# Block sums kept in PSUM banks and rotary products of 512 columns in an attention block, and the first pair's copy of P1 issued earlier

## The chip, the core and the metric

One core of a Trainium2 chip. The program is one launch; the metric is device time in microseconds of that core, median of 3 runs. Engines are named as in the profile: PE is TensorE (PEld its weight loads), DVE VectorE, ACT ScalarE, POOL GpSimd, SP SyncE, which issues loads.

## The reference, cut to what matters

```python
x = x + attn(cond(x, ids1, W1, b1, lora_As, lora_Bs), wq, wk, wv, wo)
x = x + ffn(cond2(x, ids2, W2, Wr2, A2, B2), base_w, base_b, A, Bf, router_w)

def attn(x, wq, wk, wv, wo):                     # 32 query heads, 8 key/value heads, head_dim 128, S = 64
    q, k, v = (x @ wq), (x @ wk), (x @ wv)       # reshaped to heads
    q, k = rope(q, pos), rope(k, pos)            # [t1 cos - t2 sin, t1 sin + t2 cos]
    scores = einsum("bqhgd,bshd->bhgqs", q, k) * head_dim ** -0.5
    attn = softmax(where(causal, scores, min))   # per key/value head g
    return einsum("bhgqs,bshd->bqhgd", attn, v).reshape(B, S, 4096) @ wo
```

x is 32 sequences of 64 tokens of width 1024, all in float32.

## The kernel before, in words

Tokens lie along the free axis and features along the partitions. The 2048 tokens are worked in two halves of 1024 (two tiles t = 0, 1 of NT = 512 columns), by one loop `hf` over the whole program of each engine. Each engine has its own hand-written instruction stream; nothing but semaphores orders one against another. Every float32 operand of a product is split into a high and a low part, and a product is three matmuls (`three`, L713 to L715): high by high, high by low, low by high.

The stage that the change touches lies between the first projection and the product with wo. It works through 24 pairs of heads per half (`pair(B, lp)`). Their kind goes round in threes: KV (one key and one value head), Q01 and Q23 (two query heads each). A pair is a 2 x 2 block product of Strassen's kind: seven products P1, P6, P2, P5, P7, P4, P3 in this order on PE, each 12 matmuls of 512 columns into one of four PSUM banks `prod0` to `prod3` (`BANK`: P1 and P2 share bank 2, P6 and P7 bank 3, P5 and P3 bank 1, P4 has bank 0). DVE joins them to the four result blocks: C11 = P1 + P2 lies complete in bank 2 after P2, U2 = P1 + P6, U3 = P1 + (P6 + P7), C22 = U3 + P5, C21 = U3 - P4, C12 = U2 + (P5 + P3). C11 and C12 are the two token tiles of the pair's first head, C21 and C22 those of the second. ACT makes the copy of P1 (`p1_copy`, L1339, tile `p_sum`) which U2 and U3 need; P2 overwrites nothing but adds to the same bank, so PE waits for that copy before P2.

The weights of the seven products go to seven slots: POOL forms sums of blocks (L1592), ACT rounds them to the high part (L1260, `weight_hi`), POOL subtracts for the low part (L1597).

Keys and query heads are then turned (rope): per piece two products with sin on 64 partitions each (L1901, to `rope_sin`), one with cos (L1903), and their sum (L1905) into `k_rot` or `q_rot`. Value heads are transposed on PE instead (`turn_v`).

Attention of a pair of query heads, in two units of one token tile each, is spread over the next two pairs: PE puts `score` of the first unit (16 matmuls, L897) ahead of the next pair's P6, the second one's ahead of P5, the transpose `turn_p` (L909) of the first ahead of P4 and its product with V (`pv`, L922) ahead of P3, and the second unit's at the start of the pair after. DVE masks the scores and takes the maximum (`before_exp`, L1860 to L1865), ACT takes the exponential (L1358), DVE scales (`normalise`, L1872 and L1874).

In the first pair of each half P4 needs T4, a sum that DVE makes in three steps over 2048 columns (L1839, L1841, L1844), ACT rounds (L1331) and DVE splits (`t4_lo`, L1848).

Of the kernel before, what the change touches and what calls it, by code (L numbers as in the profile page):

```python
# [130 lines left out]
def raw_count(r):  # L131
# [16 lines left out]
U2, C11, U3, C22, C21, C12 = range(1, 7)  # L148
NC = 6
# [6 lines left out]
          "s_sum": 5 * PAIRS, "unit": 4 * NKV, "tb": 6 * NKV, "qk": 8 * NKV, "raw": 16 * PAIRS // 2,  # L156
          "stored": 16 * 2 * NKV, "head": 0}
A_LOOP = {k: v * PAIRS_IT // PAIRS for k, v in A_STEP.items()}
A_LOOP["head"] = 2 * GQ
C_N = 2 * KC  # L160
# [6 lines left out]
def build(nc, x, ids1, ids2, W1, b1, A1, B1, wq, wk, wv, wo, W2, Wr2, A2, B2, Wf, bf, Af, Bf, Rf, consts,  # L167
          gates_d, m_d, c2_d, t_d, x1_d, o_d, out):
    assert D == TOK and KC == TB
    with ExitStack() as ctx:  # L170
# [161 lines left out]
        comb = sem("comb")  # L332
        roped = sem("rope_products")
# [367 lines left out]
        def _(pe):  # L701
# [83 lines left out]
            with pe.Fori(0, HALVES) as hf:  # L785
# [104 lines left out]
                def score(B, u):  # L890
# [3 lines left out]
                    pe.wait_ge(qk_in, B["qk"] + (8 * lg + 2 + 3 * (w // 2) + 2 + t))  # L894
# [32 lines left out]
                def attention(B, lp, n):  # L927

                    if lp % 3 != Q01 and lp >= 2:
                        e = 4 * ((lp - 1) // 3) + 2 * (lp % 3 == KV)  # L930
                        if n == 1:
                            score(B, e)
                        if n == 3:
                            score(B, e + 1)
                        if n == 5:
                            turn_p(B, e)
                        if n == 6:
                            pv(B, e)
                    if lp % 3 != Q23 and lp >= 3:
                        e = 4 * ((lp - 2) // 3) + 2 * (lp % 3 == Q01)  # L940
                        if n == 0:
                            turn_p(B, e + 1)
                        if n == 1:
                            pv(B, e + 1)
# [3 lines left out]
                def pair(B, lp):  # L948

                    for n in range(NP):  # L950
# [40 lines left out]
                def group(gd, par, first=False):  # L991
# [4 lines left out]
                    for i in range(32):  # L996
# [9 lines left out]
                        if first and i < 4:  # L1006

                            pe.wait_ge(comb, hf * A_STEP["comb"] + (A_STEP["comb"] - NC + (C11, U3, C21, C12)[i] + 6))
# [148 lines left out]
        def _(act):  # L1157
# [49 lines left out]
            with act.Fori(0, HALVES) as hf:  # L1207
# [1064 lines left out]
```

## Time and profile before

| | us |
|---|---|
| median of 3 runs (lowest to highest) | 2933.24 (2920.47 to 2942.37) |
| the profiled execution's own time | 2936.61 |
| its span, first to last instruction | 2934.7 |
| PE busy in the span | 2784.2 (95%) |
| DVE, POOL, ACT busy | 1770.2, 1154.9, 842.9 |
| mean granted TensorE clock, as a share of full speed | 0.964 |

The two attention stages of pairs lie at about 289 to 950 us and 1683 to 2346 us of the span. In the profile page's timeline of 40 slices PE is at 8 tenths in a few slices there and at 9 nearly everywhere else. The chain of work that ended last is 82% PE and 9% DVE.

### The profile page before, as it was taken

How to read it: one execution, taken by the hardware profiler on the slowest of the kernel's cores; microseconds unless marked ns; L12 is line 12 of the kernel's file. 1: busy time of each engine (PE TensorE's matmuls, PEld its weight loads, DVE VectorE, ACT ScalarE, POOL GpSimd, SP SyncE). 2: the span in 40 equal slices, each digit the busy share in tenths (PEclk: the TensorE clock that was granted, in tenths of full speed). 3: DMA queues.
4: the chain of work that ended last, by engine and by line, in shares of the span. 5: the costliest groups of instructions: out<-in, count | busy, mean ns of one | idle time of the engine just before them, and what ended most of it. 6: DMA issues, size and time to landing. Idle time of an engine off the chain costs nothing.

```text
span 2934.7 us, 40314 instructions
## 1 busy us (share of the span) xinstructions
PE 2784.2 (95%) x13368; PEld 2272.3 (77%) x13368; DVE 1770.2 (60%) x2187; ACT 842.9 (29%) x2019; POOL 1154.9 (39%) x678
## 2 busy tenths in 40 slices
PE   8989799999999999999998889999999999999999
PEld 7867677877777888887877667787777788887887
DVE  2133677677776766655524467767877676566452
ACT  2133234333333321121103333343333322112110
POOL 0020776666775122210303276766667412221030
PEclk9999899999999999999999999999999999999999
DMA  6861122211212332221444112212122332321232
GB/s 209 232 177 41 52 72 64 68 59 58 72 56 93 140 108 92 89 70 52 112 140 123 43 44 72 73 58 72 52 65 66 114 122 97 105 93 51 70 101 68
DMA packets 280502, 260.00 MB, mean 89 GB/s; under 512 B 67706, under 2 KB 217338, under 8 KB 280322
## 3 DMA queue, kind: packets, MB, share of 16 engines
q1 hardware_dynamic: 235106, 202.11, 23.3%
q10 hardware_dynamic: 45216, 55.58, 5.4%
q8 instruction: 102, 1.67, 0.2%
q14 instruction: 78, 0.64, 0.1%
HBM read 193.49 MB, written 64.16 MB: 88 GB/s over the span
## 4 chain that ended last, share of the span: by engine, by line
PE 82%; DVE 9%; issue 4%; POOL 2%; SPq 1%; DMA 1%; ACT 1%; DVEq 0%; POOLq 0%; ACTq 0%
PE prod L713 24%; PE prod L715 23%; PE prod L714 23%; PE turned L897 5%; DVE rope_sin L1901 2%; DVE q_rot L1903 2%; DVE q_rot L1905 2%; PE turned L922 2%; PE turned L707 1%; PE prod L1144 1%; PE turned L909 1%; POOL slot_f L1592 1%; DVE combined L1940 1%; POOL slot L1597 1%; PE prod L811 1%
## 5 line engine op out<-in xcount | busy, mean ns | idle before, releaser
L1997 DVE TENSOR_TENSOR x<-prod,x 128x512 f32<-128x512 f32 x512 | 346.8, 689 | 256.9 <-PE prod L715 256.3
L1636 POOL TENSOR_TENSOR w_lo<-raw,w_hi 128x1024 fp32r<-128x1024 f32 x64 | 157.0, 2452 | 578.1 <-ACT w_hi L1419 578.1
L713 PE MATMUL prod<-c_hi,slot 128*128 128x512 f32 x768 | 310.0, 404 | 27.6 <-ACT p_sum L1339 26.5
L713 PE MATMUL prod<-c_hi,w_hi 128*128 128x512 f32 (+1 forms) x832 | 327.3, 393 | 3.4 <-DVE c_lo L2021 3.4
L715 PE MATMUL prod<-c_hi,w_lo 128*128 128x512 f32 (+1 forms) x832 | 324.2, 390 | 0.0
L714 PE MATMUL prod<-c_lo,w_hi 128*128 128x512 f32 (+1 forms) x832 | 323.8, 389 | 0.0
L715 PE MATMUL prod<-c_hi,slot 128*128 128x512 f32 x768 | 301.5, 393 | 0.0
L714 PE MATMUL prod<-c_lo,slot 128*128 128x512 f32 x768 | 301.2, 392 | 0.0
L713 PE MATMUL prod<-x_hi,w_hi 128*128 128x512 f32 x656 | 283.4, 432 | 7.6 <-DVE w_lo L1739 2.1
L1597 POOL TENSOR_TENSOR slot<-slot_f,slot 128x512 fp32r<-128x512 f32 x144 | 212.6, 1476 | 135.4 <-ACT slot L1260 135.4
L1358 ACT ACTIVATE probs<-probs,row_max 128x64 f32<-128x64 f32 x512 | 171.0, 335 | 301.6 <-DVE row_max L1865 301.6
L715 PE MATMUL prod<-x_hi,w_lo 128*128 128x512 f32 x656 | 257.6, 393 | 0.0
L714 PE MATMUL prod<-x_lo,w_hi 128*128 128x512 f32 x656 | 256.9, 392 | 0.0
L713 PE MATMUL prod<-t_hi,slot 128*128 128x512 f32 x576 | 254.2, 441 | 1.2 <-DVE t_lo L1848 1.2
L714 PE MATMUL prod<-t_lo,slot 128*128 128x512 f32 x576 | 238.5, 414 | 0.0
L715 PE MATMUL prod<-t_hi,slot 128*128 128x512 f32 x576 | 238.5, 414 | 0.0
L897 PE MATMUL turned<-k_rot,q_rot 128*128 128x64 f32 x1024 | 151.6, 312 | 80.9 <-DVE q_rot L1905 80.9
L1901 DVE TENSOR_TENSOR rope_sin<-combined,consts_sb 64x512 f32<-64x512 f32 (+1 forms) x160 | 220.0, 1375 | 10.9
L897 PEld LDWEIGHTS turned<-k_rot,q_rot 128*128 128x128 f32 x1024 | 147.9, 226 | 96.1 <-issue 93.4
L713 PE MATMUL prod<-o_xhi,w_hi 128*128 128x512 f32 x512 | 199.3, 389 | 0.0
L715 PE MATMUL prod<-o_xhi,w_lo 128*128 128x512 f32 x512 | 199.2, 389 | 0.0
L714 PE MATMUL prod<-o_xlo,w_hi 128*128 128x512 f32 x512 | 199.2, 389 | 0.0
(176 smaller groups left out, 5328.7 us busy)
## 6 DMA issues: line engine op xcount, KB each, us to landing
o_scratch<-o_f ACTq DMA_DIRECT2D x64, 512.0 KB, 2.8
raw<-in_wo SPq DMA_DIRECT2D x64, 512.0 KB, 3.4
raw<-t_scratch SPq DMA_DIRECT2D x34, 512.0 KB, 3.5
raw_a<-in_wq SPq DMA_DIRECT2D x32, 512.0 KB, 4.7
raw<-in_wq SPq DMA_DIRECT2D x32, 512.0 KB, 4.8
c_lo_f<-o_scratch SPq DMA_DIRECT2D x32, 512.0 KB, 5.0
o_xf<-o_scratch SPq DMA_DIRECT2D x32, 512.0 KB, 5.4
t_scratch<-x ACTq DMA_DIRECT2D x17, 512.0 KB, 5.0
```

The costliest lines, as they stand in the source:

```text
L713: pe.matmul(dst, wh, xh, start=start, stop=False, skip_group_check=skip)
L714: pe.matmul(dst, wh, xl, start=False, stop=False, skip_group_check=skip)
L715: return pe.matmul(dst, wl, xh, start=False, stop=stop, skip_group_check=skip)
L897: mm = pe.matmul(SCB[:, b * SEQ:(b + 1) * SEQ], Q[:, t * 2 * NT + b * P:t * 2 * NT + (b + 1) * P], K[:, t * NT + b * SEQ:t * NT + (b + 1) ...
L922: mm = pe.matmul(OB[par][:, b * P:(b + 1) * P], V[rows, (t * BPT + b) * HD:(t * BPT + b + 1) * HD], PT[rows, b * P:(b + 1) * P], start=Tru ...
L1358: ins = act.activation(SM[:, c:c + SEQ], SM[:, c:c + SEQ], ACT.Exp, bias=MX[:, m:m + 1], scale=SM_SCALE, accum_out=SUM[:, m:m + 1])
L1597: pool.tensor_tensor(slot_lo(n), src, slot_hi(n).bitcast(F32), ALU.subtract).then_inc(s_lo, 1)
L1636: pool.tensor_tensor(WL[j % 2][:], RAW[j % 2][:], WH[j % 2][:].bitcast(F32), ALU.subtract).then_inc(split_d, 1)
L1901: dve.tensor_tensor(view(rs[a:a + hd2, :], segs), x[b:b + hd2], sin, ALU.mult)
L1903: dve.tensor_tensor(out, x, cos, ALU.mult).then_inc(signal, 1)
L1905: dve.tensor_tensor(out, out, view(rs, segs), ALU.add).then_inc(qk_in, 1)
L1997: dve.tensor_tensor(X1[:, xs], PJ[q % 4][:], X1[:, xs], ALU.add).then_inc(taken, 1)
```

## The change: what it does

Three things are changed in the pair stage.

1. For pairs of query heads, C22 is written into PSUM bank 3 and C21 into bank 0 instead of the SBUF tile `combined`; for all pairs C12 is written into bank 1. Only a value head's two blocks still go to `combined`.
2. Every rope is now of 512 columns: two per key head as before, four per pair of query heads instead of two of 512 and one of 1024 (`rope` replaces `turn`). Its source is always a PSUM bank; the product with cos overwrites that bank, after a wait for the products with sin, and the last sum reads the bank and `rope_sin`, which has two buffers in turn. C21 and C22 are turned in two ropes, C21 first.
3. Because a bank is free only when its rope is through, PE's waits ahead of P1, P6, P5 and P4 of the next pair (and ahead of the first four products of the stage after) go by `qk_in`, the count of finished ropes, instead of `comb`. Only the pairs after a KV pair keep `comb` for P6 and P4. The scores wait for the rope they need: of the first tile for the second rope, of the second tile for the fourth.

Beside that, in the first pair of each half: ACT issues `p1_copy` right after the rounding of P2's weights and not after those of P5, P7, P4, of T4 and of P3's weights; DVE makes the third step of T4 after U2 and not before it. And `attention` on PE is written with tables: where a late unit's pv and a score stand ahead of the same P6, the pv now comes first.

```diff
-U2, C11, U3, C22, C21, C12 = range(1, 7)
-NC = 6
+U2, U3, C22, C21, C12 = range(1, 6)
+NC = 5
+R11, R21, R22, R12 = range(1, 5)
...
+        def qk_count(lp, n=0):
+            return 10 * (lp // 3) + (0, 2, 6)[lp % 3] + n + 4
...
 # PE: score(B, u)
-                    pe.wait_ge(qk_in, B["qk"] + (8 * lg + 2 + 3 * (w // 2) + 2 + t))
+                    pe.wait_ge(qk_in, B["qk"] + qk_count(3 * lg + 1 + w // 2, R12 if t else R21))
...
 # PE: pair(B, lp), ahead of each product but P2
-                            last = {P1: C11 - NC, P6: U3 - NC, P5: C12 - NC, P4: C21 - NC, P7: U2, P3: C22}[n]
-                            pe.wait_ge(comb, B["comb"] + (NC * lp + last + 6))
+                            if n in (P7, P3):
+                                pe.wait_ge(comb, B["comb"] + (NC * lp + {P7: U2, P3: C22}[n] + 6))
+                            elif lp % 3 == Q01 and n in (P6, P4):
+                                pe.wait_ge(comb, B["comb"] + (NC * (lp - 1) + {P6: U3, P4: C21}[n] + 6))
+                            elif lp % 3 == Q01:
+                                pe.wait_ge(qk_in, B["qk"] + qk_count(lp - 1, {P1: 1, P5: 2}[n]))
+                            else:
+                                pe.wait_ge(qk_in, B["qk"] + qk_count(lp - 1, {P1: R11, P6: R22, P5: R12, P4: R21}[n]))
...
 # ACT, first pair of a half
-                for n in (P2, P5, P7, P4):
-                    weight_hi(B0, 0, n)
-                act.wait_ge(t4_step, hf * 4 + 3)
-                act.copy(T4H[:], T4LF[:]).then_inc(t4_hi, 1)
-                weight_hi(B0, 0, P3)
...
+                weight_hi(B0, 0, P2)
+                p1_copy(B0, 0)
+                for n in (P5, P7, P4):
+                    weight_hi(B0, 0, n)
+                act.wait_ge(t4_step, hf * 4 + 3)
+                act.copy(T4H[:], T4LF[:]).then_inc(t4_hi, 1)
+                weight_hi(B0, 0, P3)
...
 # DVE
+                    def rope(out, x):
+                        n = done[0]
+                        done[0] += 1
+                        rs = view(RS[:, (n % 2) * NT:(n % 2 + 1) * NT], SPT)
+                        x = view(x, SPT)
+                        if lp or n >= 2:
+                            dve.wait_ge(qk_in, B["qk"] + qk_count(lp, n - 1))
                         for a, b in ((0, hd2), (hd2, 0)):
-                            dve.tensor_tensor(view(rs[a:a + hd2, :], segs), x[b:b + hd2], sin, ALU.mult)
-                        dve.tensor_tensor(out, x, cos, ALU.mult).then_inc(signal, 1)
-                        dve.wait_ge(signal, value)
-                        dve.tensor_tensor(out, out, view(rs, segs), ALU.add).then_inc(qk_in, 1)
+                            ins = dve.tensor_tensor(rs[a:a + hd2], x[b:b + hd2], sin, ALU.mult)
+                        ins.then_inc(turned_sin, 1)
+                        dve.wait_ge(turned_sin, B["qk"] + (qk_count(lp, n + 1) - 4))
+                        dve.tensor_tensor(x, x, cos, ALU.mult).then_inc(roped, 1)
+                        dve.wait_ge(roped, B["qk"] + (qk_count(lp, n + 1) - 4))
+                        dve.tensor_tensor(out, x, rs, ALU.add).then_inc(qk_in, 1)
...
-                    dve.tensor_tensor(b1_, b0, bank[P5], ALU.add).then_inc(comb, 1)
+                    dve.tensor_tensor(b1_ if kind == KV else bank[P7], b0, bank[P5], ALU.add).then_inc(comb, 1)
...
-                    dve.tensor_tensor(b0, b0, bank[P4], ALU.subtract).then_inc(comb, 1)
+                    dve.tensor_tensor(b0 if kind == KV else bank[P4], b0, bank[P4], ALU.subtract).then_inc(comb, 1)
                     if kind != KV:
                         combined(C21)
-                        turn(1, both, view(CB[:, 2 * NT:4 * NT], TT * SPT), TT * SPT, 0, roped, r_of(B, lp, 1))
+                        rope(dst[0][1], bank[P4])
+                        rope(dst[1][1], bank[P7])
                     formed(P3)
-                    dve.tensor_tensor(a1, a1, bank[P3], ALU.add).then_inc(comb, 1)
+                    dve.tensor_tensor(bank[P3], a1, bank[P3], ALU.add).then_inc(comb, 1)
                     combined(C12)
-                    turn(1 if kind == KV else 2, dst[1], view(a1, SPT), SPT, 0, roped, ...)
+                    rope(dst[1][0], bank[P3])
```

DVE's stream at the end of a pair of query heads, from the sum C21 to the last rope, before (`combined` is the SBUF tile, `prod` a PSUM bank; "waits" names the semaphore of an instruction's wait):

```order
L1940 TENSOR_TENSOR combined<-combined,prod 128x512 [waits comb]
L1901 TENSOR_TENSOR rope_sin<-combined,consts_sb 64x1024 [waits qk_in]
L1903 TENSOR_TENSOR q_rot<-combined,consts_sb 128x16x64
L1905 TENSOR_TENSOR q_rot<-q_rot,rope_sin 128x16x64 [waits rope_products]
L1946 TENSOR_TENSOR combined<-combined,prod 128x512 [waits a_prod]
L1901 TENSOR_TENSOR rope_sin<-combined,consts_sb 64x512 [waits qk_in]
L1903 TENSOR_TENSOR q_rot<-combined,consts_sb 128x8x64
L1905 TENSOR_TENSOR q_rot<-q_rot,rope_sin 128x8x64 [waits rope_products]
```

The same place in the changed kernel (each `rope_sin` row stands twice in both kernels and is shown once; the rope of C22 reads like that of C21, its first row is shown):

```order
L1965 TENSOR_TENSOR prod<-combined,prod 128x512 [waits comb]
L1921 TENSOR_TENSOR rope_sin<-prod,consts_sb 64x512 [waits qk_in]
L1925 TENSOR_TENSOR prod<-prod,consts_sb 128x512 [waits turned_sin]
L1927 TENSOR_TENSOR q_rot<-prod,rope_sin 128x8x64 [waits rope_products]
L1921 TENSOR_TENSOR rope_sin<-prod,consts_sb 64x512 [waits qk_in]
L1971 TENSOR_TENSOR prod<-combined,prod 128x512 [waits a_prod]
```

The one rope of 1024 columns has become two of 512, and no rope instruction reads two SBUF tiles any longer.

ACT's stream at the first pair of a half, before, from the rounding of P2's weights (`slot_96`) on:

```order
L1260 CAST slot_96<-raw_88 128x512 [waits c_prod,a_raw0]
L1260 CAST slot_97<-slot_f_104 128x512 [waits s_sum]
L1260 CAST slot_98<-slot_f_105 128x512 [waits s_sum]
L1260 CAST slot_99<-raw_89 128x512 [waits c_prod,a_raw1]
L1331 CAST t_hi<-t_lo_f 128x2048 [waits t4_step]
L1260 CAST slot_100<-slot_f_107 128x512 [waits s_sum]
L1339 COPY p_sum<-prod 128x512 [waits comb]
```

And in the changed kernel:

```order
L1274 CAST slot_96<-raw_88 128x512 [waits c_prod,a_raw0]
L1346 COPY p_sum<-prod 128x512 [waits comb]
L1274 CAST slot_97<-slot_f_104 128x512 [waits s_sum]
L1274 CAST slot_98<-slot_f_105 128x512 [waits s_sum]
L1274 CAST slot_99<-raw_89 128x512 [waits c_prod,a_raw1]
L1441 CAST t_hi<-t_lo_f 128x2048 [waits t4_step]
L1274 CAST slot_100<-slot_f_107 128x512 [waits s_sum]
```

The copy of P1 has moved ahead of five rounding steps, the rest keeps its order.

## Rows read from the trace of the kernel before

**Rows 1.** Waits: who waited for whom, us in total, times, longest.

```profile
PE turned L897 <- DVE q_rot L1905: 80.9, 30, 3.7
PE prod L713 <- ACT p_sum L1339: 26.5, 2, 13.2
```

**Rows 2.** Windows: length; busy PE, PEld, DVE, ACT, POOL; clock; DMA.

```profile
289.00:950.00 661.00, 605.55 (x3095) 498.99 (x3094) 483.22 (x517) 244.99 (x767) 446.47 (x285) 0.93 0.21 65
950.00:1555.00 605.00, 596.60 (x2706) 484.17 (x2704) 344.81 (x502) 119.53 (x166) 106.88 (x42) 0.99 0.33 102
1683.00:2346.00 663.00, 610.27 (x3111) 503.18 (x3112) 476.78 (x521) 248.32 (x776) 445.65 (x284) 0.93 0.22 67
```

**Rows 3.** Timeline of PE: start, duration, line, tiles, [idle before <- releaser].

```profile
504.44 0.39 PE L715 MATMUL prod<-t_hi,slot 128*128 128x512 f32 x1
...
513.99 3.67 PE L897 MATMUL turned<-k_rot,q_rot 128*128 128x64 f32 x16 [3.34 <-DVE q_rot L1905]
...
517.99 0.63 PE L714 MATMUL prod<-t_lo,slot 128*128 128x512 f32 x1
...
524.42 1.89 PE L897 MATMUL turned<-k_rot,q_rot 128*128 128x64 f32 x16
...
544.02 3.31 PE L897 MATMUL turned<-k_rot,q_rot 128*128 128x64 f32 x16 [1.72 <-DVE q_rot L1905]
```

**Rows 4.** Timeline of DVE, from C21 of a Q01 pair to its last rope.

```profile
504.95 0.69 DVE L1940 TENSOR_TENSOR combined<-combined,prod 128x512 f32<-128x512 f32 x1 [1.22 <-PE prod L715]
505.76 3.61 DVE L1901 TENSOR_TENSOR rope_sin<-combined,consts_sb 64x1024 f32<-64x1024 f32 x2
509.38 2.22 DVE L1903 TENSOR_TENSOR q_rot<-combined,consts_sb 128x1024 f32<-128x1024 f32 x1
511.63 2.17 DVE L1905 TENSOR_TENSOR q_rot<-q_rot,rope_sin 128x1024 f32<-128x1024 f32 x1
...
517.18 1.67 DVE L1903 TENSOR_TENSOR q_rot<-combined,consts_sb 128x512 f32<-128x512 f32 x1
518.88 0.69 DVE L1905 TENSOR_TENSOR q_rot<-q_rot,rope_sin 128x512 f32<-128x512 f32 x1
```

**Rows 5.** Timeline of POOL in the same stretch, two rows that follow each other.

```profile
516.58 1.72 POOL L1597 TENSOR_TENSOR slot<-raw_a,slot 128x512 fp32r<-128x512 f32 x1
524.52 1.28 POOL L1597 TENSOR_TENSOR slot<-s_f,slot 128x512 fp32r<-128x512 f32 x1 [6.22 <-ACT slot L1260]
```

**Rows 6.** Groups by form: count, busy us, mean ns, idle before.

```profile
L897 PE MATMUL turned<-k_rot,q_rot 128*128 128x64 f32 x1024 | 151.6, 312 | 80.9 <-DVE q_rot L1905 80.9
...
L1901 DVE TENSOR_TENSOR rope_sin<-prod,consts_sb 64x512 f32<-64x512 f32 x96 | 66.1, 688 | 97.8 <-PE prod L715 96.9
...
L1903 DVE TENSOR_TENSOR q_rot<-prod,consts_sb 128x512 f32<-128x512 f32 x32 | 22.1, 692 | 0.4
```

**Rows 7.** Timeline of all engines in the first pair of half 1.

```profile
297.17 2.54 POOL L1597 TENSOR_TENSOR slot<-slot_f,slot 128x512 fp32r<-128x512 f32 x1 [0.73 <-ACT slot L1260]
298.62 3.24 DVE L1844 TENSOR_TENSOR t_lo_f<-t_hi_f,t_lo_f 128x2048 f32<-128x2048 f32 x1
...
303.71 1.27 POOL L1597 TENSOR_TENSOR slot<-slot_f,slot 128x512 fp32r<-128x512 f32 x1 [0.73 <-ACT slot L1260]
304.06 1.89 ACT L1331 CAST t_hi<-t_lo_f 128x2048 fp32r<-128x2048 f32 x1
...
307.98 0.58 ACT L1339 COPY p_sum<-prod 128x512 f32<-128x512 f32 x1
...
308.61 0.80 PE L713 MATMUL prod<-c_hi,slot 128*128 128x512 f32 x1 [13.23 <-ACT p_sum L1339]
...
316.25 3.38 DVE L1848 TENSOR_TENSOR t_lo<-t_lo_f,t_hi 128x2048 fp32r<-128x2048 f32 x1
```

**Rows 8.** Timeline of DVE and PE: normalise of a unit, and the transpose it feeds.

```profile
529.27 1.79 DVE L1874 TENSOR_TENSOR probs<-probs,row_rcp 128x512 f32<-128x512 f32 x1
...
531.70 0.60 PE L909 MATMUL turned<-consts_sb,probs 128*128 128x128 f32 x4
```

More of the change, by code:

```diff
@@ L155 @@
 A_STEP = {"a_prod": NP * PAIRS, "comb": NC * PAIRS, "p1s": PAIRS, "s_hi": NP * PAIRS, "s_lo": NP * PAIRS,
-          "s_sum": 5 * PAIRS, "unit": 4 * NKV, "tb": 6 * NKV, "qk": 8 * NKV, "raw": 16 * PAIRS // 2,
+          "s_sum": 5 * PAIRS, "unit": 4 * NKV, "tb": 6 * NKV, "qk": 10 * NKV, "raw": 16 * PAIRS // 2,
           "stored": 16 * 2 * NKV, "head": 0}
@@ L159 @@
 A_LOOP["head"] = 2 * GQ
+SCORE_AT = (1, 3)
+TURN_AT = (5, 7)
+PV_AT = (6, 8)
 C_N = 2 * KC
@@ L332, in build @@
         comb = sem("comb")
+        turned_sin = sem("turned_sin")
         roped = sem("rope_products")
@@ L927, in attention @@
                 def attention(B, lp, n):
[L929 to L944, printed above, removed]
+                    for late in (1, 0):
+                        src = lp - 1 - late
+                        if src >= 1 and src % 3 != KV:
+                            e = 4 * (src // 3) + 2 * (src % 3 == Q23)
+                            for i in range(2):
+                                if PV_AT[i] == n + 7 * late:
+                                    pv(B, e + i)
+                                if SCORE_AT[i] == n + 7 * late:
+                                    score(B, e + i)
+                                if TURN_AT[i] == n + 7 * late:
+                                    turn_p(B, e + i)
                     if lp % 3 == Q01 and n in (2, 3):
@@ L1006, in group @@
                         if first and i < 4:
-                            pe.wait_ge(comb, hf * A_STEP["comb"] + (A_STEP["comb"] - NC + (C11, U3, C21, C12)[i] + 6))
+                            pe.wait_ge(qk_in, hf * A_STEP["qk"] + qk_count(PAIRS - 1, (R11, R22, R21, R12)[i]))
                         q = Q_G + i
@@ L1382, in pair @@
                         weight_hi(B, lp, P3)
-                    p1_copy(B, lp)
+                        p1_copy(B, lp)
                     if not last:
@@ L1661, in _ @@
             dve.sem_inc(comb, 6)
+            dve.sem_inc(qk_in, 4)
             def wf_lo(b):
@@ L1842, in _, with t4_sum @@
                                   view(CL[:].bitcast(F32), KC)[:, b21, 0:NT], ALU.subtract).then_inc(t4_step, 1)
-                dve.wait_ge(t4_step, t4 + 2)
-                dve.tensor_tensor(T4LF[:], T4HF[:], T4LF[:], ALU.add).then_inc(t4_step, 1)
+                def t4_sum():
+                    dve.wait_ge(t4_step, t4 + 2)
+                    dve.tensor_tensor(T4LF[:], T4HF[:], T4LF[:], ALU.add).then_inc(t4_step, 1)
                 def t4_lo():
@@ L1884, in pair @@
                     host = 4 * ((lp - 1) // 3) + 2 * (kind == KV) if kind != Q01 and lp >= 2 else None
-                    qk = 8 * lg + (0, 2, 5)[kind]
+                    done = [0]
                     def formed(n):
@@ L1907, in pair @@
                     if kind == KV:
-                        dst = [view(K[:, t * NT:(t + 1) * NT], SPT) for t in range(TT)]
+                        dst = [[view(K[:, t * NT:(t + 1) * NT], SPT)] for t in range(TT)]
                     else:
-                        dst = [Q[:, t * 2 * NT:(t + 1) * 2 * NT].rearrange("p (s h q) -> p h s q", s=SPT, h=2)[:, 0]
-                               for t in range(TT)]
+                        dst = [[Q[:, t * 2 * NT:(t + 1) * 2 * NT].rearrange("p (s h q) -> p h s q", s=SPT, h=2)[:, h]
+                                for h in range(2)] for t in range(TT)]
@@ L1917, in pair @@
                     dve.tensor_tensor(a1, P1S[:], bank[P6], ALU.add).then_inc(comb, 1)
+                    if lp == 0:
+                        t4_sum()
                     formed(P2)
-                    turn(0, dst[0], view(bank[P2], SPT), SPT, 1, comb, B["comb"] + (NC * lp + C11 + 6))
+                    rope(dst[0][0], bank[P2])
                     if host is not None:
@@ L1964, in _ @@
                 B = a_bases(dve, hf, 0, A_NAMES)
-                B["roped"] = dve.snap(hf * (5 * NKV))
                 for lp in range(2):
```

15 lines of the change are left out of this document (2 added, 13 removed).

## The prediction, as recorded before the run

> **What bounds the kernel now.** First the page's shares: PE is busy 95% of the span, so a gain must come out of PE's own idle time, out of its clock, or out of its work. The change leaves PE's matmuls as they are, so only the first two are left. Then the view of waits for PE: two entries stand out, 80.9 us in 30 waits of the scores (L897) for DVE's last rope sum, and 26.5 us in 2 waits of a product for the copy of P1 [rows 1]. Together 107 us, and the change is aimed at both. Then the windows: in the two pair stages the granted clock is 0.93, in the stage between them 0.99 [rows 2]; some of the loss in the pair stages is clock. The timeline of PE shows where: after the 3.34 us gap the score group takes 3.67 us, against 1.89 for one with no gap ahead of it, and the product matmuls behind it stand at 0.63 us instead of 0.39 for a while (one start every 0.43 instead of 0.23 us: 1.2 GHz instead of 2.4) [rows 3]. In both stages no such stretch stands without a gap shortly ahead; after gaps of 1.72 us it follows some times (3.31 us at 544.02 [rows 3]) and others not.
>
> Why does the score wait? A score of the first token tile needs two heads of that tile, and the second head's comes out of the 1024 column rope. DVE's rows of one Q01 pair: C21 starts at 504.95, the rope of 1024 runs 505.76 to 513.80 (3.61 + 2.22 + 2.17), the score starts 0.19 later [rows 3, 4]. PE stood ready at 513.99 - 3.34 = 510.65. Per column these instructions cost more than those that read PSUM: 3.61 us for two of 1024 is 0.9 us per 512, 2.22 us is 1.11, against 0.688 and 0.692 us for 512 columns out of a bank [rows 4, 6]. It isn't the memory as such: at 517.18 a cos product from SBUF takes 1.67 us while POOL has a subtraction from 516.58 to 518.30, and at 518.88 the sum of two SBUF tiles takes 0.69 us, when POOL stands still until 524.52 [rows 4, 5]. So two SBUF inputs are slowed by POOL; one PSUM input and one SBUF input are not, whatever POOL does (688 ns is the mean of 96).
>
> **The change part by part, first the ropes.** New rope of 512 columns: sin twice 2 x 0.69, cos 0.69, sum 0.69, some 0.15 in issue and own waits (before, 0.12 between C21's end and the rope, 0.03 between others [rows 4]): 2.85 us. The wait for the sin products ahead of cos is of the same kind as the old one ahead of the sum, which costs 0.02 to 0.04: I cost it at nothing more. From P4's end at 504.83 [rows 3]: C21 504.95 to 505.64, its rope to 508.5, C22's to 511.4, C12's sum to 512.1, its rope to 515.0 (before: 519.57).
>
> - Score of the first tile: needs C21's rope, 508.5 + 0.2, PE comes at 510.65. The wait goes, with 2 us to spare. In the other place (Q23 to KV, the gaps of 1.72) P3 has a pv ahead, so PE comes later still; it goes too.
> - P6 of the next pair now waits for C22's rope, which it did not before: 511.4 + 0.2 = 511.6, PE comes at 510.65 + 1.70 = 512.35. It holds by 0.7 us. This is the tightest new wait.
> - Score of the second tile and P5 wait for C12's rope, 515.0; PE comes two products (5.5 us) later, near 518. P4 and P1 wait for ropes that are done long before.
> - The scores' masking, done by DVE in order behind C12's rope, begins at about 515.1 instead of 519.6; the exponentials start earlier, all in front of what PE needs.
>
> Worth: 80.9 us of idle. Score groups: 64 groups are 151.6 us busy [rows 6], at 1.89 they would be 121.0: 30.6 us. Products: I count 182 slow ones behind the 30 gaps, 0.20 us each: 36 us. Check: (0.99 - 0.93) x 1324 us is 79 us of lost clock [rows 2], 67 of it found so in work and some in the gaps themselves. Sum 147.5 us.
>
> DVE: a Q pair saves 2.5 us at the wide rope (8.0 to 5.6) and 2.3 at the last, a KV pair about 2.3; with 16 and 8 pairs per half some 190 us less busy in all. It was 483 us of 661 busy [rows 2], not the bound, and this in itself is worth nothing. POOL meets fewer two-input instructions and gets shorter; its work is hidden too.
>
> **First pair of a half.** Before: the 13.23 us gap ends with the P1 copy at 307.98, which stood in ACT's queue behind T4's rounding at 304.06 [rows 7]. P6 ended at 308.61 - 13.23 = 295.38, and P1 a product of 12 x 0.23 us earlier, at 292.6; so the copy now runs at once and P2 follows P6 without a gap. What is late next: P5 waits for POOL's low part, 299.71; P7 for the next one, 303.71 + 1.27 = 304.98; P4 for T4's low part. T4's third step (3.24) comes after U2 now, 299.4 to 302.6, ACT's rounding (1.89) still at about 304.2 behind POOL-bound casts, the rope of C11 fits before it, then 3.38 for the low part: 309.5 [rows 7]. P4 starts at 309.7 instead of 320.0 (316.25 + 3.38 and its 1.2 us gap). So of 13.23 us 10.3 are saved, and the pair behind can follow at once: POOL fills its seven slots in about 12 x 1.27 + 4 x 0.73 = 18 us, PE empties them in 84 x 0.23 = 19.3, and POOL starts some 5 us ahead. Gaps of about 1.9, 2.5 and 1.8 us remain and may bring some slow clock, as the old gap did. I take 10.3 x 2 = 20.5 us, between 12 (gaps bring the clock down) and 24.
>
> **New cost at the stage's end.** The following stage's second product waits for C22's rope: 6.8 us after P4's end against 5.6 at which PE comes: 1.2 us a half, 2.4. Order of pv and score within one place: nothing, the same work in one queue.
>
> **Sum.** 147.5 + 20.5 - 2.4 = 165.6 us off the profiled execution's 2936.6: 2771. The median of the runs is 3.4 us lower, so 2768; I add 4 us for small new waits that such a compressed schedule finds: **2772 us**.
>
> **The unknown price: writing a PSUM bank from DVE.** No row of the trace shows it; every DVE instruction there writes SBUF. Nearest are the same instructions reading a bank, 688 to 692 ns [rows 6]; I take that for both. Lower end: nothing gained below it, since SBUF-only instructions take 0.69 too at their best. Upper end, an instruction twice as long, 1.38, if read and write of the same bank take turns: three such lie ahead of C22's rope after P4 (C21, two cos), 2.1 us late, minus the 0.7 in hand: 1.4 us of gap at 16 places, 22 us, and up to 3.4 us of clock with each, 54 us more: 2795 to 2850.
>
> A rule of the Trainium skill speaks against the change here. "VectorE: DVE Perf Modes", section on the TRN2 errata, gives VectorE 58 cycles beside the columns for an SBUF source and 120 for PSUM, and its rules for kernel authors advise a copy to SBUF first where many operations follow on a matmul's output. By it each of the nine instructions up to C22's rope would take 65 ns more, an estimate of 0.6 us, leaving 0.1 of the 0.7 in hand and the sum where it is. The trace disagrees with the 65 ns: 688 ns out of a bank [rows 6], 0.69 us for two SBUF tiles with POOL idle [rows 4].
>
> **The rivals.**
> - *PSUM writes are dear, P6 waits* (chance 0.12): as worked out, 2795 to 2850. For it: P6's reserve is only 0.7 us. Against: nothing in the rows makes a bank slower than SBUF.
> - *The softmax becomes the wait* (0.10): turn_p of the first unit waits for DVE's normalise, which ended at 531.06; PE came at 531.70 [rows 8]. In hand 0.6 us, and this chain (rope of C11, masking, normalise, all after P2) does not get shorter, PE's part neither. If it slips by 1 us at 32 units, 32 us: about 2800. For it: normalise still has two SBUF inputs and took 1.79 us. Against: the rope of C11 costs the same as before.
> - *The scores wait for something else* (0.04): if the mask of the unit before or the clock by itself holds them, only the first pair's 20 us come: 2905 to 2920.
> - *Slower* (0.04): DVE becomes the bound. Three pairs take 661 / 8 = 82.6 us and DVE is busy 60.4 of them [rows 2], about 48.5 after. They hold 17 instructions that write a bank. With x us more for each, DVE needs 48.5 + 17x; it passes 82.6 from x = 2.0, an instruction of 2.7 us. At x = 2.5 it is 91, and 16 such rounds make +134, less the first pair's 20: about 3050. For it: the price is unseen. Against: it needs four times what any bank access in the trace takes.
>
> The forecast has the rest, 0.70, in 2756 to 2790: the low end where the first pair gives its 24 us and no small waits appear. The range must leave out no more than 2 in 10, so it takes in the first two rivals for the most part: **2755 to 2830**. A measurement tells about 1% here, 29 us, from no change. Faster by over 1%: 0.70 + 0.12 + 0.10 and none of the rest, 0.92. Within: 0.04. Slower: 0.04.
>
> **What would show it.** In the changed profile: PE's waits for DVE's rope at the scores gone, and no new one above some us at P6; cos products `prod<-prod` at about 0.69 us; score groups near 1.9 us all through; granted clock in the pair stages at 0.97 or more; P2 of each first pair right behind P6, with three gaps of 2 us behind; DVE busy near 1580 us. Wrong would be: `prod<-prod` above 1 us, waits of products for `q_rot`, or of the transposes for `probs`, or a clock that stays at 0.93 without gaps.

## The result and the profile after

| | before | after |
|---|---|---|
| median, us (lowest to highest) | 2929.65 (2920.47 to 2942.37), 4 runs | 2782.96 (2781.59 to 2785.98), 4 runs |
| ratio of the times, 95% interval | | 0.9498 (0.9459 to 0.9536) |
| the profiled execution, us | 2936.6 | 2786.0 |
| span; PE busy; PE idle, us | 2934.7; 2784.2; 150.5 | 2784.2; 2713.7; 70.5 |
| mean granted TensorE clock | 0.964 | 0.992 |

Faster by 5.0%. The forecast of 2772 was 11 us too low, and the range, 2755 to 2830, held the time. Of the 150.5 us by which the span shrank, 80.0 are idle time of PE and 70.5 are matmuls that took less time.

Waits of PE in the changed kernel, as in [rows 1]: who waited for whom, us in total, times, longest.

```profile
PE prod L725 <- ACT p_sum L1346: 12.6, 2, 6.3
...
PE prod L725 <- POOL slot L1611: 9.3, 6, 2.3
PE prod L725 <- DVE q_rot L1927: 6.0, 2, 3.0
...
PE turned L934 <- ACT probs_t L1359: 2.2, 2, 1.1
PE turned L921 <- DVE probs L1891: 1.9, 4, 0.7
```

The 30 waits of the scores, 80.9 us [rows 1], have no row any more. The copy of P1 still costs 12.6 us, and two waits are new: 9.3 us for POOL's low parts and 6.0 us for a rope.

Windows over the two stages of pairs, as in [rows 2]: length; busy PE, PEld, DVE, ACT, POOL; clock; DMA.

```profile
291.00:881.00 590.00, 576.03 (x3142) 476.44 (x3141) 399.04 (x586) 251.51 (x780) 380.70 (x286) 0.99 0.25 79
...
1602.00:2193.00 591.00, 578.33 (x3141) 478.65 (x3140) 397.69 (x585) 251.59 (x780) 381.23 (x286) 0.99 0.25 78
```

A stage takes about 590 us, where it took 661, and the clock is 0.99 in it as it was in the stage between [rows 2]. In the page's timeline of the kernel before, the slice with the first stage's first pair stands at 7 tenths, lower than the section on the profile before says.

The groups by form that answer to [rows 6]: count, busy us, mean ns, idle before.

```profile
L909 PE MATMUL turned<-k_rot,q_rot 128*128 128x64 f32 x1024 | 122.6, 273 | 0.0
...
L1921 DVE TENSOR_TENSOR rope_sin<-prod,consts_sb 64x512 f32<-64x512 f32 x320 | 220.3, 689 | 94.8 <-PE prod L727 80.9 <-DVE prod L1971 1.9
...
L1925 DVE TENSOR_TENSOR prod<-prod,consts_sb 128x512 f32<-128x512 f32 x160 | 112.0, 700 | 5.6
L1927 DVE TENSOR_TENSOR q_rot<-prod,rope_sin 128x512 f32<-128x512 f32 x128 | 88.6, 692 | 4.4
```

The score groups are 122.6 us where they were 151.6. The unseen price shows in the third row: an instruction that reads a bank and writes the same bank takes 700 ns, against 689 and 692 for its neighbours that read a bank and write SBUF.

The end of a Q01 pair on DVE, as in [rows 4], from C21 to C12's sum.

```profile
562.04 0.70 DVE L1965 TENSOR_TENSOR prod<-combined,prod 128x512 f32<-128x512 f32 x1 [1.14 <-PE prod L727]
562.86 1.39 DVE L1921 TENSOR_TENSOR rope_sin<-prod,consts_sb 64x512 f32<-64x512 f32 x2
564.28 0.70 DVE L1925 TENSOR_TENSOR prod<-prod,consts_sb 128x512 f32<-128x512 f32 x1
565.02 0.69 DVE L1927 TENSOR_TENSOR q_rot<-prod,rope_sin 128x512 f32<-128x512 f32 x1
565.74 1.39 DVE L1921 TENSOR_TENSOR rope_sin<-prod,consts_sb 64x512 f32<-64x512 f32 x2
567.16 0.70 DVE L1925 TENSOR_TENSOR prod<-prod,consts_sb 128x512 f32<-128x512 f32 x1
567.90 0.69 DVE L1927 TENSOR_TENSOR q_rot<-prod,rope_sin 128x512 f32<-128x512 f32 x1
568.51 0.69 DVE L1971 TENSOR_TENSOR prod<-combined,prod 128x512 f32<-128x512 f32 x1
```

PE at the same place, as in [rows 3]: the score of the first tile and the first matmul of P6.

```profile
567.19 1.89 PE L909 MATMUL turned<-k_rot,q_rot 128*128 128x64 f32 x16
...
568.89 0.48 PE L725 MATMUL prod<-t_hi,slot 128*128 128x512 f32 x1
```

C21's rope ends at 565.71, the score starts at 567.19 with no wait: 1.5 us to spare, 2 were forecast. C22's rope ends at 568.59, P6 starts 0.30 later, and no wait stands before it.

ACT at the start of the first half, with the first and the second pair's copy of P1 (`p_sum`).

```profile
294.40 0.59 ACT L1346 COPY p_sum<-prod 128x512 f32<-128x512 f32 x1 [0.98 <-PE prod L727]
...
324.62 0.61 ACT L1274 CAST slot<-raw_a 128x512 fp32r<-128x512 f32 x1
328.52 0.62 ACT L1274 CAST slot<-slot_f 128x512 fp32r<-128x512 f32 x1 [3.29 <-POOL slot_f L1606]
329.05 0.58 ACT L1346 COPY p_sum<-prod 128x512 f32<-128x512 f32 x1
```

POOL in the same stretch: the first instruction for the second pair's slots, the sum that ACT's rounding at 328.52 waits for, and the last low part.

```profile
313.18 1.29 POOL L1606 TENSOR_TENSOR s_f<-raw_a,raw_a 128x512 f32<-128x512 f32 x1
...
327.23 1.26 POOL L1606 TENSOR_TENSOR slot_f<-raw_a,s_f 128x512 f32<-128x512 f32 x1
329.22 1.27 POOL L1611 TENSOR_TENSOR slot<-slot_f,slot 128x512 fp32r<-128x512 f32 x1 [0.73 <-ACT slot L1274]
```

PE in the same stretch: the three gaps in the first pair, the start of the second, and its P2.

```profile
301.49 0.49 PE L725 MATMUL prod<-t_hi,slot 128*128 128x512 f32 x1 [1.76 <-POOL slot L1611]
...
306.78 0.49 PE L725 MATMUL prod<-c_hi,slot 128*128 128x512 f32 x1 [2.27 <-POOL slot L1611]
...
310.43 0.49 PE L725 MATMUL prod<-t_hi,slot 128*128 128x512 f32 x1 [0.65 <-DVE t_lo L1865]
...
317.21 0.49 PE L725 MATMUL prod<-c_hi,slot 128*128 128x512 f32 x1 [0.86 <-POOL slot L1611]
...
329.68 0.79 PE L725 MATMUL prod<-c_hi,slot 128*128 128x512 f32 x1 [6.28 <-ACT p_sum L1346]
```

In the first pair P4 starts at 310.43 instead of 320.0. The second pair's P2 then waits 6.28 us: PE stood ready at 323.40, but ACT has that copy in its queue behind the rounding of P3's weights, which waits for POOL's sum until 328.5. Before, the same copy ran at almost the same time of the span:

```profile
328.58 0.59 ACT L1339 COPY p_sum<-prod 128x512 f32<-128x512 f32 x1 [0.79 <-PE prod L715]
```

There it waited for PE's P1, not for POOL. From one pair's first matmul to the next one's, the first pair takes 26.3 us where it took 36.2, and the second 28.6 where it took 20.0: the second gave back 8.5 of the 10.0 that the first gained.

### The profile page after: what moved, and what is told of

Its sections match the earlier page's. It is cut to its first block, busy times and chain, and to the rows that moved or that the text cites. A ratio compares the mean times of both kernels' runs of the same rounds, so it can differ in the third digit from the quotient of the medians.

```text
span 2784.2 us, 40365 instructions
## 1 busy us (share of the span) xinstructions
PE 2713.7 (97%) x13368; PEld 2218.7 (80%) x13368; DVE 1592.3 (57%) x2315; ACT 844.6 (30%) x2019; POOL 1016.2 (36%) x678
## 4 chain that ended last, share of the span: by engine, by line
PE 90%; issue 3%; POOL 2%; DVE 2%; SPq 2%; DMA 1%; ACT 1%; POOLq 0%; ACTq 0%; DVEq 0%
PE prod L725 26%; PE prod L727 26%; PE prod L726 26%; PE turned L909 4%; PE turned L934 2%; PE turned L719 1%; PE prod L1158 1%; POOL slot_f L1606 1%; PE turned L921 1%; POOL slot L1611 1%; PE prod L823 1%; PE prod L771 1%; PE turned L899 0%; PE prod L1135 0%; SPq L509 0%
## 5 line engine op out<-in xcount | busy, mean ns | idle before, releaser
L725 PE MATMUL prod<-c_hi,slot 128*128 128x512 f32 x768 | 310.9, 405 | 20.0 <-ACT p_sum L1346 12.6
L1921 DVE TENSOR_TENSOR rope_sin<-prod,consts_sb 64x512 f32<-64x512 f32 x320 | 220.3, 689 | 94.8 <-PE prod L727 80.9
L725 PE MATMUL prod<-t_hi,slot 128*128 128x512 f32 x576 | 237.5, 412 | 4.2 <-POOL slot L1611 3.5
L1611 POOL TENSOR_TENSOR slot<-slot_f,slot 128x512 fp32r<-128x512 f32 x144 | 188.4, 1308 | 138.3 <-ACT slot L1274 138.3
L727 PE MATMUL prod<-t_hi,slot 128*128 128x512 f32 x576 | 226.3, 393 | 0.0
L726 PE MATMUL prod<-t_lo,slot 128*128 128x512 f32 x576 | 224.9, 391 | 0.0
L725 PEld LDWEIGHTS prod<-c_hi,w_hi 128*128 128x128 f32 (+1 forms) x832 | 155.5, 187 | 46.1 <-DVE q_rot L1927 6.8
L725 PEld LDWEIGHTS prod<-c_hi,slot 128*128 128x128 f32 x768 | 145.4, 189 | 55.9 <-ACT p_sum L1346 13.0
```

The lines of the kernel that those rows point to most:

```text
L725: pe.matmul(dst, wh, xh, start=start, stop=False, skip_group_check=skip)
L726: pe.matmul(dst, wh, xl, start=False, stop=False, skip_group_check=skip)
L727: return pe.matmul(dst, wl, xh, start=False, stop=stop, skip_group_check=skip)
L1611: pool.tensor_tensor(slot_lo(n), src, slot_hi(n).bitcast(F32), ALU.subtract).then_inc(s_lo, 1)
L1921: ins = dve.tensor_tensor(rs[a:a + hd2], x[b:b + hd2], sin, ALU.mult)
```

## The experiments

The medians of the kernel before beside them were 2935.18 us in the first group (the first four), 2932.77 in the second (the next four), and 2933.64 in the third. All ratios are against the kernel before.

**The ropes alone** (`ropes_only`): the changed kernel with ACT's order in the first pair, and T4's third step, as before.

```diff
-                weight_hi(B0, 0, P2)
-                p1_copy(B0, 0)
-                for n in (P5, P7, P4):
+                for n in (P2, P5, P7, P4):
                     weight_hi(B0, 0, n)
...
                 weight_hi(B0, 0, P3)
+                p1_copy(B0, 0)
```

> The changed kernel with the first pair of each half as before (copy of P1 behind the rounding of T4 and of P3's weights, T4's third step ahead of the loop). Theory from the changed profile: the early copy gained only what the new gaps and the 6.28 us wait in the second pair left of the 13.2 us gap, 4 to 6 us a half, so this kernel takes 2783 + 9 = 2792 us. Rival, my prediction's term: the early copy is worth 20 us, so 2803. In both the score waits stay away and the granted clock in the later pairs is near 1.

Measured: 2783.35 us (2779.41 to 2786.37), ratio 0.9480 (0.9457 to 0.9504), the time of the whole change. The wait for the first pair's copy stands there in full and costs nothing against the changed kernel:

```profile
PE prod L725 <- ACT p_sum L1346: 26.4, 2, 13.2
```

Both expected times, 2792 and the rival's 2803, were missed. The first two pairs together show the same in the trace: 55.1 and 56.1 us in the two halves here, 54.8 and 55.6 in the changed kernel, 0.7 us less in all. It follows that the ropes bring the 150 us, and the early copy, on top of them, next to nothing.

**The early copy alone** (`copy_only`): the kernel before with that order.

```diff
+                weight_hi(B0, 0, P2)
+                p1_copy(B0, 0)
+                for n in (P5, P7, P4):
+                    weight_hi(B0, 0, n)
...
+                    if lp == 0:
+                        t4_sum()
```

> The kernel before with the early copy of P1 and the later third step of T4 alone. Theory: the parts add up, 2930 - 9 = 2921 us, with the 30 score waits at 80 us in all as before. Rival: the early copy is worth its 20 us here, 2910. A second rival, that the score waits take the gain back: 2930.

Measured: 2937.77 us (2923.06 to 2946.5), ratio 1.0002 (0.9981 to 1.0024). The scores' waits are untouched, and the wait for P1's copy has only moved to the second pair:

```profile
PE turned L897 <- DVE q_rot L1908: 80.7, 30, 3.7
PE prod L713 <- ACT p_sum L1333: 15.1, 2, 7.6
```

From the start of one pair's first product to the next one's, the first two pairs took 36.2 and 20.0 us before, and 26.7 and 30.6 here. Their sum grows from 56.3 to 57.3. The expected 2921 us did not come. The time is that of the second rival, but not its reason: the scores' waits took nothing back, the second pair did.

**Sums in SBUF, ropes as in the change** (`sums_in_sbuf`): four ropes of 512 columns in the new order with the new waits, but C21, C22 and C12 go to `combined`, and so sin and cos products and the last sum read SBUF alone. One more wait on `qk_in` guards the reuse of `combined` ahead of U2. P6 still waits for C22's rope, as in the changed kernel, though C22 now lies in SBUF; in the kernel before it waited for U3 alone.

```diff
-                    dve.tensor_tensor(b1_ if kind == KV else bank[P7], b0, bank[P5], ALU.add).then_inc(comb, 1)
+                    dve.tensor_tensor(b1_, b0, bank[P5], ALU.add).then_inc(comb, 1)
...
-                        rope(dst[0][1], bank[P4])
-                        rope(dst[1][1], bank[P7])
+                        rope(dst[0][1], b0)
+                        rope(dst[1][1], b1_)
```

> The changed kernel with the block sums C21, C22 and C12 in the SBUF tile again and all ropes still of 512 columns with the cos product in place there (PE's waits unchanged). Theory, it is the two SBUF inputs that cost, through POOL: a rope takes 4 to 5 us instead of 2.85, C21's is through about when PE reaches the score, C22's 3 us after PE reaches P6: 16 gaps of about 3 us with slow clock behind, 2850 to 2885 us, rope rows of SBUF at 1.1 to 1.7 us. Rival, the narrow rope in front does it all: 2783 to 2790 us and no waits.

Measured: 2954.61 us (2952.61 to 2956.86), ratio 1.0069 (1.0046 to 1.0092): all of the gain is gone, and a little more. Waits of PE, and DVE's groups by form, of this kernel:

```profile
PE prod L725 <- DVE q_rot L1927: 105.1, 32, 4.6
...
PE turned L909 <- DVE q_rot L1927: 7.6, 13, 0.7
```

```profile
L1921 DVE TENSOR_TENSOR rope_sin<-combined,consts_sb 64x512 f32<-64x512 f32 x224 | 246.9, 1102 | 8.1
L1925 DVE TENSOR_TENSOR combined<-combined,consts_sb 128x512 f32<-128x512 f32 x112 | 148.7, 1328 | 3.9
...
L1921 DVE TENSOR_TENSOR rope_sin<-prod,consts_sb 64x512 f32<-64x512 f32 x96 | 66.1, 688 | 86.4 <-PE prod L727 85.5
```

The same line, shape and program: a mean of 1102 ns with two SBUF inputs, 688 with one of them in a bank. Sorted by what POOL does meanwhile, the 1102 come apart: 60 of the 224 meet no POOL instruction and take 685 ns on average, 92 have POOL beside them for more than 80% of their time and take 1543. Of the 96 with a bank as source it is 690 ns without POOL and 686 beside it. So what makes the rope long is two SBUF inputs at a time when POOL works.

The time was 70 us above the expected 2850 to 2885, which reckoned with 16 gaps of 3 us. There are 30 at P6 in the pairs, 4.6 us each behind Q01 pairs and 2.2 behind Q23 pairs for the most part, and 2 of 3.4 us at the stage's end. The granted clock of the stage falls back to 0.94 with them. The waits of the scores, however, are not back: 7.6 us in 13 places, where the kernel before had 80.9 in 30. With the rope of 512 columns and the earlier C21 most of the old waits are gone even with SBUF sources (the holds at P6, which give DVE time, may help), and the loss sits at P6, which is held until C22's rope is through. That hold is needed only where C22 lies in the bank. A kernel with SBUF sums, narrow ropes and P6's old wait was not run, so what the narrower ropes are worth by themselves stays open. What is shown: under the changed kernel's waits, the gain hangs on the source in PSUM.

**Cos product to SBUF** (`cos_to_sbuf`): it is written to `q_rot` as before, and the last sum has two SBUF inputs.

```diff
-                        dve.tensor_tensor(x, x, cos, ALU.mult).then_inc(roped, 1)
+                        dve.tensor_tensor(out, x, cos, ALU.mult).then_inc(roped, 1)
...
-                        dve.tensor_tensor(out, x, rs, ALU.add).then_inc(qk_in, 1)
+                        dve.tensor_tensor(out, out, rs, ALU.add).then_inc(qk_in, 1)
```

> The changed kernel with the cos product written to the query tile in SBUF instead of back to the bank; the last sum of a rope then has two SBUF inputs. Theory: that sum takes up to 1.67 us instead of 0.69 while POOL works, C22's rope ends up to 2 us later, P6 waits some 1.2 us at 16 places, 2800 to 2830 us. Rival, writing a bank in place is worth nothing: 2783.

Measured: 2804.49 us (2802.76 to 2806.36), ratio 0.9558 (0.9537 to 0.9580). Its last sum, and P6's wait:

```profile
L1927 DVE TENSOR_TENSOR q_rot<-q_rot,rope_sin 128x512 f32<-128x512 f32 x128 | 144.8, 1131 | 4.4
```

```profile
PE prod L725 <- DVE q_rot L1927: 15.2, 17, 2.9
```

The time is in the expected range. The sum takes 1131 ns instead of 692, and P6 waits at 15 more places, 0.2 to 0.8 us each. Writing the bank in place is worth 21 us; the other 150 between this kernel and `sums_in_sbuf` are those of the bank as a source, under the same waits.

**P6's reserve** (`late_1`, `late_9`): ahead of C22's rope DVE makes one unused product of 64 x 512, which takes 0.68 us, and in `late_9` eight more of 64 x 64, which take 1.22 us together (each is 0.23 us long, but they overlap). C22's rope is thus 0.7 and 1.9 us later, not the 2.4 that the expectation of `late_9` took.

```diff
+                        if kind != KV and n == 2:
+                            dve.wait_ge(qk_in, B["qk"] + qk_count(lp, n))
...
+                            dve.tensor_tensor(other[0:hd2], x[0:hd2], cos, ALU.mult)
+                            for e in range(8):       # late_1: range(0)
+                                dve.tensor_tensor(RS[hd2:P, NT + e * SEQ:NT + (e + 1) * SEQ], x[hd2:P, e],
+                                                  CT[hd2:P, C_COS:C_COS + SEQ], ALU.mult)
```

> The changed kernel with one more product of 64 x 512 out of the bank (0.69 us, its result unused) ahead of C22's rope in every pair of query heads. Theory: PE reaches P6 about 0.7 us after C22's rope is through, so this is just hidden: 2783 to 2790 us and waits at P6 under 0.2 us. Rival, the reserve is larger or nothing waits for C22's rope: exactly 2783 and no wait. Rival, DVE's time counts as such: 32 x 0.69 = 22 us, 2805.

> The same with nine unused products, one of 64 x 512 and eight of 64 x 64, about 2.4 us. Theory: at the 16 places behind a Q01 pair P6 waits 1.7 us, at the 16 behind a Q23 pair it is hidden by 3 us of reserve: 27 us, and slow clock behind a part of the gaps, 2810 to 2840 us. Rival, hidden altogether: 2783. Rival, DVE's time counts at all 32 places: 2860.

Measured: `late_1` 2790.28 us (2790.01 to 2791.96), ratio 0.9525 (0.9493 to 0.9557); `late_9` 2825.39 us (2821.66 to 2827.18), ratio 0.9639 (0.9606 to 0.9672). The first matmul of P6 behind a Q01 pair, of `late_1` and then of `late_9`, a place of each:

```profile
567.27 0.50 PE L725 MATMUL prod<-t_hi,slot 128*128 128x512 f32 x1 [0.26 <-DVE q_rot L1935]
```

```profile
1682.34 0.79 PE L725 MATMUL prod<-t_hi,slot 128*128 128x512 f32 x1 [1.50 <-DVE q_rot L1935]
```

In `late_1` C22's rope ends at 567.21 and the matmul starts 0.06 later; in the changed kernel that distance is 0.30. P6 thus has 0.30 - 0.06 = 0.24 us in hand, not 0.7. The round of three pairs says the same: mostly 72.60 us in the changed kernel and 73.09 in `late_1`, so 0.49 of the 0.69 us of delay came through; 12 places have the wait, some 6 us in all, and `late_1` is 7.3 and 4.2 us above the two measurements of the changed kernel. Its waits of 0.26 us are a little over the 0.2 expected. In `late_9` the waits behind the Q01 pairs sum to 31.3 us less 9.7 at the stage's ends, 21.6 in 16 places. The time grew by 39 us over that of `after_again` (below), within the expected range. Between the profiles of these two, PE was busy 17.2 us more (2728.2 against 2711.0) and idle 23.2 us more. The busy part is slower matmuls behind the waits: behind 7 of the 16 places matmuls run at half the clock for a while, in 4 of them from the first on (0.79 us in the row), and the mean clock of the span is 0.986 against 0.991.

**The second pair's copy moved ahead of P3's rounding** (`copy2_first`: in the second pair; `copies_first`: in all but the first).

```diff
                     if lp:
-                        weight_hi(B, lp, P3)
                         p1_copy(B, lp)
+                        weight_hi(B, lp, P3)
```

> The changed kernel with the copy of P1 put ahead of the rounding of P3's weights on ACT in the second pair of a half alone. Theory: the wait of 6.28 us in the second pair comes from that order and goes, but in the third pair the same order holds the copy behind POOL's sum again, about 2.5 us: 2783 - 2 x 4 = 2775 us. Rival, POOL itself is behind and the wait moves to a weight slot: 2783.

> The same order in all pairs but the first. Theory: all waits for the copy go, 2783 - 12.6 = 2770 us. Rival, P3's low weights come late in other pairs since POOL's queue is held by the later rounding: 2783 or slower.

Measured: 2787.15 us (2786.66 to 2789.55), ratio 0.9515 (0.9488 to 0.9543), and 2788.62 (2787.55 to 2789.53), 0.9517 (0.9490 to 0.9544): not faster than the change, where 2775 and 2770 were expected. The first two pairs took 57.6 and 57.4 us in `copy2_first`, 56.5 and 57.1 in `copies_first`, more than the 54.8 and 55.6 of the changed kernel. Waits of PE in `copy2_first`:

```profile
PE turned L899 <- ACT v_tok L1351: 8.0, 2, 4.0
PE prod L725 <- ACT p_sum L1346: 4.8, 2, 2.4
```

The wait for the copy shrank from 6.3 to 2.4 us and the next thing in ACT's queue took its place: the copies of V's transposes (`take_v`), which stand behind further roundings that wait for POOL. One move within ACT's queue isn't enough.

**ACT's whole order at the first two pairs** (`act_order`): the second pair's P1 copy comes at the end of the first pair's work, ahead of P3's rounding and right behind that of P5; both V copies come at the start of the second pair; from the third pair on P1's copy precedes P3's rounding.

```diff
-                    if lp:
+                    if lp == 1:
+                        take_v(B, 0, 0)
+                        take_v(B, 0, 1)
                         weight_hi(B, lp, P3)
+                    if lp > 1:
                         p1_copy(B, lp)
+                        weight_hi(B, lp, P3)
...
                         weight_hi(B, lp + 1, P5)
+                        if lp == 0:
+                            p1_copy(B, 1)
```

> The changed kernel with another order on ACT in the first two pairs of a half: the second pair's copy of P1 ahead of the rounding of P7's and P4's weights, and its two copies of V ahead of the rounding of P3's and of the third pair's weights. Theory: POOL's own queue would let PE go on, it is ACT that stands behind POOL with work that PE waits for; with that work in front, the first two pairs take about 47 us instead of 54.9, 2783 - 16 = 2767 us. Rival: POOL is the bound of the first pairs whatever ACT's order, as with the two reorderings before: 2783 to 2788, and a wait in the third pair.

> The changed kernel once more, as the measure for the three beside it on the same chip: 2783 us, within 5.

Measured: `act_order` 2767.68 us (2761.98 to 2770.65), ratio 0.9434 (0.9414 to 0.9455); the changed kernel again, in the same group, 2786.10 (2781.66 to 2787.41), 0.9496 (0.9476 to 0.9516). The second P1 copy of `act_order`:

```profile
317.47 0.58 ACT L1346 COPY p_sum<-prod 128x512 f32<-128x512 f32 x1
```

It is 11.6 us earlier in the span than at 329.05, and 7.7 us earlier when both are counted from the first pair's start (287.05 and 290.95). The first two pairs take 26.2 and 20.1 us (the changed kernel: 26.3 and 28.6), no wait for the copy is left, and 18 us are won: about 2 x 8.5. 2767 was expected. So the loss in the second pair was ACT's order, not POOL's pace.

**C22's rope ahead of C21's** (`c22_first`), right behind C22's sum, since P6 waits for it first; and both together (`act_order_c22`).

```diff
-R11, R21, R22, R12 = range(1, 5)
+R11, R22, R21, R12 = range(1, 5)
...
+                    if kind != KV:
+                        combined(C22)
+                        rope(dst[1][1], bank[P7])
```

> The changed kernel with C22's rope made before P4 is awaited, C21's after it. Theory: PE's wait of 3.0 us for a rope in the stage after (once a half) goes at least in part, since C22's rope is then made before DVE's work for that stage, 2783 - 4 = 2779 us; everywhere else nothing changes. Rival: C21's rope, now behind, becomes late in the last pair, and the masks too: 2783 or up to 5 more.

> Both of these together. Theory: they are in different places and add, 2763 us. Rival: as far as one of them fails, 2767 or 2779.

Measured: `c22_first` 2780.41 us (2779.04 to 2783.11), ratio 0.9482 (0.9462 to 0.9501); `act_order_c22` 2762.46 (2761.53 to 2764.69), 0.9419 (0.9400 to 0.9437). Waits in `c22_first`:

```profile
PE prod L725 <- DVE c_lo L1983: 3.3, 2, 1.7
PE turned L909 <- DVE q_rot L1927: 2.4, 12, 0.2
```

The two waits of 3.0 us at the stage's end are gone and 1.7 us for `c_lo` stands there; the reserve has passed from P6 to the scores, which now wait 0.2 us at 12 places. From the last pair's start on, 200 matmuls take 3.4 us less in each half than in `after_again`, and the pairs before it about 2 us more in each: about 3 us, as the profiled spans differ (2781.3 and 2784.6). The medians differ by 5.7 us, with intervals that overlap, so alone this is hardly above the noise. Together with ACT's order it is the best version: 24 us below the changed kernel, with intervals far apart, and 171 us below the kernel before.

## Why the prediction was right, and where it was off

- **Scores and clock, 147.5 us: right.** `ropes_only` has it without the first pair: 2935.2 to 2783.4, 151.8 us, with the new waits at the stage's end already paid (147.5 - 2.4 = 145.1 forecast for both). The idle part is the 80.9 us; PE's busy time fell by 78.1 there and by 70.5 in the whole change, where 30.6 + 36 = 66.6 were forecast. The clock of the stages is 0.99, and with no wait left at the scores (0.0 us idle before L909) the rival "the scores wait for something else" fell. `late_9` shows the link the other way: waits put back bring slow matmuls behind some of them.
- **The unknown price: right.** Taken as 688 to 692 ns, it is 700. The rival of dear PSUM writes falls on this row.
- **Two SBUF inputs beside POOL: right**, by `sums_in_sbuf`: 1543 ns beside POOL, 685 without it. The Trainium skill states the rule ("SBUF — State Buffer", section "Who interferes with whom"): a VectorE instruction with two SBUF inputs contends with GpSimd's reads, one with at most one SBUF input does not. The rows agree, 1543 beside POOL against 686 with one input in a bank. Whether the scores' waits needed the bank is another matter: with SBUF sources and the narrow, earlier rope they are 7.6 us of the old 80.9, so part of the 80.9 may be owed to the rope's width and place and not to its source; the runs don't part the two. No run here tries the rule of the Trainium skill that the prediction cites ("VectorE: DVE Perf Modes", rules for kernel authors: a copy to SBUF first where many operations follow on a matmul's output); nearest is `sums_in_sbuf`, 171 us slower under the changed kernel's waits.
- **The first pair, 20.5 us: wrong, it brought 0.7** (`ropes_only`). The step that failed is "the pair behind can follow at once". Its numbers held: POOL began the second pair's slots at 313.18, 4 us ahead of PE at 317.21, and was through at 330.5, 17.3 us later (18 forecast). What it left out is that PE doesn't only need slots: it needs the P1 copy at 323.4, a third of the way into the pair, and ACT has that behind the rounding that waits for one of POOL's last sums. The prediction read ACT's queue for the first pair and not for the second. `act_order` gets 18 us, by putting the second pair's copy in front. The stated time survived this only because the range is wide: with this term at nothing the forecast would have been 2792, which it also holds.
- **The stage's end, 2.4 us: too small, 6.0.** C21 was put 0.1 us behind P4's end. In the last pair alone DVE has two splits for the next stage ahead of it (3.9 us), and C21 starts 3.5 us behind P4's end at 875.99:

```profile
875.64 3.88 DVE L1981 TENSOR_TENSOR c_lo<-c_lo_f,c_hi 128x1024 fp32r<-128x1024 f32 x2 [0.57 <-ACT c_hi L1434]
879.44 0.68 DVE L1965 TENSOR_TENSOR prod<-combined,prod 128x512 f32<-128x512 f32 x1
```

- **P6's reserve, 0.7 us: 0.24.** C22's rope is through 6.7 us behind P4's end (561.91), as forecast; PE comes 7.0 us behind it and not 7.5, in part because a pause of 0.24 us that stood ahead of the next pair's P1 before (starts at 507.16 and 507.63, where 0.23 lies between others) is gone. The sign held, so it cost nothing, but by little: three instructions that write a bank lie ahead, and 0.08 us more for each would have used it up. What the rival would have cost is about what `late_9` shows, 16 gaps of 1.35 us on average for 39 us; it was priced at 22 to 76.
- **Softmax wait:** PE's waits for `probs` are 1.9 us in 4 places, before and after. The rival fell.
- **DVE busy** 1592 us, near 1580 forecast.

In sum, of the 165.6 us forecast (4 us for unnamed small waits not taken off) 99.0 were idle time of PE (80.9 + 20.5 - 2.4) and 66.6 work; the span lost 80.0 and 70.5. The idle part is 80.9 of the scores and 13.9 of the P1 copies (26.5 became 12.6), less 9.3 for POOL's slots, 6.0 for ropes at the stage's end and 1.9 more for `probs_t`: 77.6, and 2.4 in waits too small to name. The 19.0 us of idle time missing are 15.9 of the first pair's 20.5 (20.5 less 13.9 - 9.3 = 4.6; even these did not shorten the time, since PE was busy 7.6 us longer than in `ropes_only`), 3.6 at the stage's end and 1.9 for `probs_t`, less the 2.4. With 3.9 us more of work saved than forecast, the span fell short by 15; 4 of them were allowed for, and 11 remain.

## What to carry to other kernels

When VectorE works beside a busy GpSimd, give each two-tensor instruction one operand in PSUM, in place if need be, and look at the mean of one form with either source before pricing it. Count what the bank costs too: it stays taken until its last reader is through, and each product that waits for it needs a reserve. When a wait is taken away, follow each in-order queue that feeds the stretch through the next two rounds: what the early engine meets next is often an instruction parked behind another engine's work. A stage's last round has work of the next stage in its queues; price it by its own rows.

## What the runs showed of the hardware beside that

- A query rope's sum of 128 x 512 with two SBUF inputs has a mean of 1131 ns in `cos_to_sbuf`, 693 where no POOL instruction overlaps it and 1459 where POOL works for over 80% of it, and of 692 with one input in PSUM. POOL is slowed too: its subtraction of the same size has a mean of 1308 ns in the changed kernel and 1475 in `sums_in_sbuf`. Beside a 2048-column instruction of DVE for T4 (`t4_lo`, 307.66 to 310.05) a POOL sum of that size takes far longer than the 1.26 to 1.30 us of those in the next pair:

```profile
307.85 3.34 POOL L1606 TENSOR_TENSOR slot_f<-raw,s_f 128x512 f32<-128x512 f32 x1
```

- Waits of 0.26 us ahead of P6 (`late_1`) leave the granted clock where it was; of the 16 waits of 0.65 to 1.5 us in `late_9`, 7 are followed by matmuls at half the clock (one start every 0.43 us instead of 0.23) and 9 are not; the gaps of 1.72 us before the change were of both kinds too [rows 3].
